# Third stage of an eight-part fused network: routing ahead of the base product, bias as a product, deltas added by accumulating transfers

## The reference, cut to what matters

```
# layer 2 (the third)
y2   = grouped_conv1d(x, 9 taps) + ctx[:, :, None] + bias
base = y2 @ base_w.T + base_b                      # 2048 x 1024 x 1024
h    = y2 @ A.T                                    # rank 64
probs = softmax(y2 @ router_w.T); topw, topi = top_k(probs, 2)
delta = sum over the 2 chosen experts e: topw_e * (h @ B[e].T)     # 16 experts
x    = x + base + 0.5 * delta
# layer 3 (the fourth)
y3 = per-sample 64x64 mix of x + bias
x  = x + layernorm(relu(y3 @ up)**2 @ down + gated latent path) * gamma + beta
```

## Time and profile before

| | us |
|---|---|
| median of 3 runs (lowest to highest) | 1807.75 (1804.79 to 1808.0) |
| profiled execution: its own time | 1816.88 |
| profiled execution: span of the trace | 1815.2 |
| PE busy, share of the span | 1644.1, 91% |
| DVE, ACT, POOL busy | 839.6, 500.3, 423.2 |

### The profile page before, as it was taken

One profiled execution on the slowest core, in us unless ns is written; L12 is line 12 of the kernel. 1 busy time (PEld: TensorE's weight loads), 2 busy tenths in 40 slices (PEclk: granted clock), 3 DMA queues, 4 the chain that ended last, 5 costly groups with the idle time before them and its releaser, 6 DMA issues.

```text
span 1815.2 us, 20711 instructions
## 1 busy us (share of the span) xinstructions
PE 1644.1 (91%) x7830; PEld 1326.3 (73%) x7830; DVE 839.6 (46%) x1294; ACT 500.3 (28%) x763; POOL 423.2 (23%) x272
## 2 busy tenths in 40 slices
PE   6799678999897978776899999999999999999997
PEld 3688546988875646655678888888767888888875
DVE  5455458995274433654523333333282333333326
ACT  2344223333225332110032222221243222222112
POOL 1000111234245244555611111111251111111110
PEclk9999889999997988878999999999999999999999
DMA  8577444457831355455621111111462111111114
GB/s 280 132 176 168 152 77 151 161 179 234 312 141 53 115 214 197 165 187 202 232 91 47 47 47 46 46 46 47 134 214 70 47 47 47 46 46 46 47 58 162
DMA packets 108210, 222.82 MB, mean 123 GB/s; under 512 B 21892, under 2 KB 60924, under 8 KB 107260
## 3 DMA queue, kind: packets, MB, share of 16 engines
q1 hardware_dynamic: 86612, 161.00, 27.9%
q0 software_dynamic: 13120, 38.88, 6.6%
q10 hardware_dynamic: 8400, 21.89, 3.7%
HBM read 152.96 MB, written 76.61 MB: 126 GB/s over the span
## 4 chain that ended last, share of the span: by engine, by line
PE 67%; DMA 7%; DVE 4%; POOL 3%; issue 2%; ACT 2%; SPq 1%; another core or an unknown queue 1%; ACTq 0%; POOLq 0%; DVEq 0%
PE pd L1775 25%; PE pu L1775 24%; PE pf L1775 6%; PE l_po L1775 4%; DMA delta<-scratch_expert_out 3%; PE pw L390 2%; PE pw L391 2%; POOL l_x L1371 1%; PE l_ea L1213 1%; DMA scratch_expert_out<-expert_out,pair_rows 1%; PE l_po L1714 1%; DMA l_y<-scratch_y2T 1%; DMA pair_rows<-scratch_pairs 1%; PE pg L997 1%
## 5 line engine op out<-in xcount | busy, mean ns | idle before, releaser
L1910 POOL TENSOR_TENSOR down_lo<-raw,down_hi 128x1024 fp32r<-128x1024 f32 x40 | 100.3, 2508 | 698.2 <-ACT down_hi L1923 698.2
L1775 PE MATMUL pd<-down_hi,hid_hi 128*128 128x512 f32 x640 | 249.1, 389 | 2.9 <-issue 2.9
L1775 PE MATMUL pu<-y_hi,up_hi 128*128 128x512 f32 x640 | 249.2, 389 | 0.0
L1775 PE MATMUL pu<-y_hi,up_lo 128*128 128x512 f32 x640 | 249.0, 389 | 0.0
L1775 PE MATMUL pd<-down_hi,hid_lo 128*128 128x512 f32 x640 | 249.0, 389 | 0.0
L1775 PE MATMUL pd<-down_lo,hid_hi 128*128 128x512 f32 x640 | 249.0, 389 | 0.0
L1775 PE MATMUL pu<-y_lo,up_hi 128*128 128x512 f32 x640 | 249.0, 389 | 0.0
L2079 DVE TENSOR_TENSOR hid_lo<-hidden,hid_hi 128x512 fp32r<-128x512 f32 x64 | 44.3, 692 | 393.3 <-ACT hid_hi L1987 393.3
L2018 DVE TENSOR_TENSOR acc<-pd,acc 128x512 f32<-128x512 f32 x224 | 143.6, 686 | 54.7 <-PE pd L1775 51.4
L1981 ACT ACTIVATE hidden<-pu 128x512 f32<-128x512 f32 x64 | 38.3, 598 | 464.9 <-PE pu L1775 464.9
L1775 PEld LDWEIGHTS pd<-down_hi,hid_hi 128*128 128x128 f32 x640 | 120.2, 188 | 28.6 <-issue 3.7
(11 more groups left out here) (306 smaller groups left out, 2689.4 us busy)
## 6 DMA issues: line engine op xcount, KB each, us to landing
X<-scratch_x SPq DMA_DIRECT2D x256, 64.0 KB, 2.6
l_x<-scratch_x SPq DMA_DIRECT2D x32, 512.0 KB, 5.8
delta<-scratch_expert_out SPq DMA_DIRECT2D x32, 512.0 KB, 7.2
raw<-in_up SPq DMA_DIRECT2D x32, 512.0 KB, 3.7
raw<-in_down SPq DMA_DIRECT2D x32, 512.0 KB, 4.2
x_in<-in_x SPq DMA_DIRECT2D x16, 512.0 KB, 4.7
scratch_x<-x_in SPq DMA_DIRECT2D x16, 512.0 KB, 4.4
scratch_x<-l_x SPq DMA_DIRECT2D x16, 512.0 KB, 5.6
```

Source lines behind the costliest of these rows:

```text
L1775: mm = pe.matmul(out, lhs[a], rhs[b], start=first and n == 0, stop=last and n == len(pairs) - 1)
L1910: pool.tensor_tensor(dn[u][i][1][:], raw[i][:], dn[u][i][0][:].bitcast(F32), ALU.subtract).then_inc(dn_lo, 1)
```

## The change

**Order.** On PE the last conv tile and the last two router products come ahead of the second half of base tile 0, and `rank_pairs` behind base chunk (1, 0). DVE runs `choose` right after the last conv output. Only base tiles 0 to 5 and the first half of 6 stand ahead of the experts; the second half of tile 6 is spread over the first nine expert groups, three matmuls at a time; nine steps follow, with base tiles 7 to 15, and the mixes start one step later.

**Loads.** `y2` is loaded in halves, the expert matrices in eight pieces of 1 MB by SP instead of four of 2 MB by ACT, and split with one copy per expert instead of two. ACT issues `mats_in`, POOL the stores of y3.

**Experts.** Row numbers travel as floats and are copied out of the group's buffer (`row_numbers`), and the pair rows are copied twice side by side (`pair_rows_twice`), so a group's buffer is free once both copies are made; one transpose of 128 columns replaces a transpose and a matmul. The outputs alternate between two pairs of banks instead of three.

**Bias.** Two matmuls per tile with 33 rows add `base_b` in place of POOL's 16 additions.

**Deltas.** `deltas_in`, `delta_sum` and `add_deltas` are gone. POOL issues two accumulating transfers per tile from the expert rows onto the tile of `x`; from tile 7 on `base_out` comes behind them. Beta is no longer added in this stage but by an accumulating transfer onto the loaded `x3b` slot in the fourth stage.

```diff
+        all_expert_rows(pool)
+        for t in range(NT + 1):
+            if t < NT:
+                if t < 7:
+                    pool.wait_ge(x3p_made, 2 * (t + 1))
+                else:
+                    pool.wait_ge(x3_loaded[t % 4], 16 * (t // 4 + 1))
+                pool.dma_start(x3[t][:], SC["eo"][t * P:(t + 1) * P, :], accum_op=ALU.add).then_inc(first_added[t % 2], 16)
+            if t:
+                last = t - 1
+                pool.wait_ge(first_added[last % 2], 16 * (last // 2 + 1))
+                if last >= 2:
+                    pool.wait_ge(second_added[last % 2], 16 * (last // 2))
+                pool.dma_start(x3[last][:], SC["eo"][(NT + last) * P:(NT + last + 1) * P, :], accum_op=ALU.add).then_inc(
+                    second_added[last % 2], 16)
+            if t >= 13:
+                y3_out(t - 5)
...
         def rows_in(g):
-            n = min(4, NEXP - 4 * g)
             if g >= 3:
-                sp.wait_ge(tr_mm, g - 2)
-                for sem in eo_stored:
-                    sp.wait_ge(sem, 16 * (g - 2))
+                sp.wait_ge(twice, g - 2)
+                sp.wait_ge(row_ids, g - 2)
...
+        def x3_again(t):
+
+            old = t - 9
+            sp.wait_ge(x3b_stored[old % 4], 16 * (old // 4 + 1))
+            sp.wait_ge(y_mm, 2 * (old + 1))
+            x3_in(t)
...
         def base_out(t):
+            dve.wait_ge(x3_loaded[t % 4], 16 * (t // 4 + 1))
             dve.wait_ge(base_mm, 2 * (t + 1))
-            dve.wait_ge(xb, t + 1)
+            if t >= 7:
+                dve.wait_ge(second_added[t % 2], 16 * (t // 2 + 1))
...
+        def base_bias(t):
...
+            for h in range(2):
+                last = pe.matmul(po[t % 2][h][:], K["ones_r"][0:BR, :], brow[:, chunk(h)], start=False, stop=True)
+            last.then_inc(base_mm, 1)
...
         base_chunk(0, 0)
         prior["conv"](pe, NT - 2)
         router(pe, NT - 3)
-        base_chunk(0, 1)
         prior["conv"](pe, NT - 1)
         router(pe, NT - 2)
+        router(pe, NT - 1)
+        base_chunk(0, 1)
         base_chunk(1, 0)
-        router(pe, NT - 1)
+        rank_pairs()
         base_chunk(1, 1)
-        base_chunk(2, 0)
-        rank_pairs()
-        base_chunk(2, 1)
-        for t in range(3, 8):
+        for t in range(2, 6):
             base_chunk(t, 0)
             base_chunk(t, 1)
+        base_chunk(6, 0)
         turn_rows(0)
...
         for g in range(NGRP):
             if g + 1 < NGRP:
                 turn_rows(g + 1)
-            for i in range(4 * g, min(4 * g + 4, NEXP)):
-                expert_tile(i)
-        for b in range(8):
-            if b == 0:
-                pe.wait_ge(eo_act, NEXP)
-                pe.wait_ge(eo_dve, NEXP)
-            base_chunk(8 + b, 0)
-            base_chunk(8 + b, 1)
-            mix(2 * b)
-            mix(2 * b + 1)
+            for n in range(rows_of(g)):
+                expert_tile(4 * g + n)
+            if g == 0:
+                base_start(6, 1)
+            if g < 8:
+                base_part(6, 4 + g // 2, g % 2)
+            if g == 8:
+                base_bias(6)
+        for s in range(9):
+            base_chunk(7 + s, 0)
+            base_chunk(7 + s, 1)
+            for t in mixed_tiles(s):
+                mix(t)
...
+        def add_beta(T):
+            pool.wait_ge(x3b_loaded[T % 2], 16 * (T // 2 + 1))
+            pool.dma_start(x3b[:, T % 2, :], A["L3_ffn_ln_beta"].partition_broadcast(P), accum_op=ALU.add).then_inc(beta_added[T % 2], 16)
...
                     pool.wait_ge(out_made, T + 1)
                     pool.dma_start(tile_of(out, T), acc[:, t, :]).then_inc(out_stored, 16)
+                    if t + 2 < HT:
+                        add_beta(T + 2)
```

More of the change, by code:

```diff
@@ L1141, in phase_l2 @@
 def phase_l2(nc, K, A, SC, s_, buf, first, prior):
[L1146 to L1150, removed]
+    B, B_raw, y2s, y2, war, blank, lg, below, every, pos, expert_of, ids, G, Gd, res, brow, brow_raw, bias_tmp, val, taken, pick = [buf[n] for n in (
+        "B B_raw y2s y2 war blank lg below every pos expert_of ids G Gd res brow brow_raw bias_tmp val taken pick").split()]
+    half_tmp, rT, eo, x3, mats, bias3, y3, y, y_raw, ea, tr, po = [buf[n] for n in (
+        "half_tmp rT eo x3 mats bias3 y3 y y_raw ea tr po").split()]
+    ge, key, lg2, ex, posf, steps, count, steps_int, pair_int, compare, prod = [buf[n] for n in (
+        "ge key lg2 ex posf steps count steps_int pair_int compare prod").split()]
     m, kmax, m2, e2, z, tot, w, tiles, scan1, scan2 = [buf[n] for n in "m kmax m2 e2 z tot w tiles scan1 scan2".split()]
@@ L1156, in phase_l2 @@
     po = [po[0:2], po[2:4]]
-    out_banks = [ea, po[0], po[1]]
+    out_banks = [ea, po[1]]
     py = [ea, tr]
     R1A, R1B, R2A = 15, 23, 36
[L1161 to L1164, removed]
@@ L1288, in sync @@
         sp.wait_ge(r_mm, NT)
+        sp.wait_ge(val_stored, 16 * 2 * NT)
+        for g in range(3):
+            rows_in(g)
+        sp.wait_ge(B_rest, E2)
         x3_in(6)
-        x3_in(7)
[L1291 to L1297, removed]
-        x3_in(8)
@@ L1299, in sync @@
[L1299 to L1306, removed]
-        for b in range(8):
[L1308 to L1313, removed]
+        y2_in(7, 0)
@@ L1314, in sync @@
+        for g in range(3, NGRP):
+            rows_in(g)
+            if g == 6:
+                y2_in(7, 1)
+        y2_in(8, 0)
+        sp.wait_ge(tr_mm, NGRP)
+        x3_in(7)
+        sp.wait_ge(twice, NGRP)
+        sp.wait_ge(row_ids, NGRP)
+        x3_in(8)
+        y2_in(8, 1)
+        for s in range(9):
+            if 9 + s < NT:
+                y2_in(9 + s, 0)
+            elif 9 + s == NT:
                 sp.wait_ge(y2_lo, 2 * NT)
                 first["raw"](sp, 0)
-                sp.wait_ge(xb, NT)
@@ L1666, in tensor, with base_part, base_start @@
     def tensor(pe):
-        def base_chunk(t, c):
+        def base_part(t, k, h):
+            return split_product(pe, po[t % 2][h][:], [v[:, k * P:(k + 1) * P] for v in y2s],
+                                 [v[:, k, chunk(h)] for v in base], k == 0, False)
+        def base_start(t, c):
             if c == 0:
@@ L1697, in turn_rows @@
                 pe.wait_ge(route, R2A)
[L1698 to L1701 removed]
+            for n in range(rows_of(g)):
+                last = pe.transpose(tr[g % 2][:, n * P:(n + 1) * P], Gd[:, g % 2, n, :, :].rearrange("p u r -> p (u r)"), K["ident"][:])
             last.then_inc(tr_mm, 1)
```

442 lines of the change are left out of this document (241 added, 201 removed).

## The result

| | us, median (lowest to highest) | ratio to before, 95% interval |
|---|---|---|
| before | 1807.9 (1804.8 to 1810.2) | |
| changed | 1783.3 (1777.0 to 1785.7) | 0.986 [0.9829, 0.989] |
| forecast | 1728 (range 1695 to 1772) | 0.956 |

What follows compares the result with a forecast made beforehand. PE gaps in the third stage, from waits for `y2` and deltas, were taken as the bound. Third stage -87, fourth +7: -80, 1816.9 to 1737 profiled; with the median 9.1 lower, 1728 us, range 1695 to 1772.

Steps and rivals of the forecast that it cites:

- The fourth stage ... +7: Fourth stage: adding beta between a slot's load and use costs +4 at the first half's end, +3 at the program's end.
- first base chunk: Start of the base work in the third stage, taken at 471.15 us as origin for all new times.
- expert stores, first to last: Third stage, experts: 6.4 to 6.7 us per four tiles, 11.5 times, 75 us against 97.1 before.
- to the end of the stage: Third stage from base tile 9 at 690: 1.5 half clock, 115.5 for seven steps, 6 for DMA, ending at 813.
- step from profile to median: The median of runs taken as 9.1 us below the profiled execution, as in the kernel before.
- the order up to the first scatter: Third stage, start: reordered PE work and earlier `choose` put the first pair scatter at 506.8 us, against 532.5.
- the one stall before base tile 9: Third stage: PE waits 23 us for `y2_low`, queued on DVE behind tile 7's `base_out` and its deltas.
- Gaps in the expert beat: Sign of being wrong: expert stores not keeping the even beat of 6.4 to 6.7 us per four.
- The deltas: Third stage: two accumulating transfers per tile, 4.5 us taken between 2.9 (cost like plain) and 5.9 (cost double).
- A landing of an accumulating transfer beyond 8 us: Sign of being wrong: any accumulating transfer taking over 8 us to land.
- At nothing: POOL's 16 bias and 16 beta additions: Third stage: removing these additions priced at no gain, since only the first tiles' bias was ever waited for.
- PE starving during the scatter: Rival, chance 0.15: PE's wait around the pair scatter returns at some 535 to 550 us, +16, total 1744.

Runs made afterwards that it cites:

- run 1: Changed kernel without the sixteen accumulating transfers of beta, so the output lacks beta; 1744.8 us, ratio to before 0.9542.
- run 4: Kernel before with only beta moved, from POOL's additions in the third stage to accumulating transfers in the fourth; 1831.0 us, ratio to before 1.0022.
- run 6: Changed kernel with beta accumulated onto the stored x3b in DRAM instead of the loaded slot; 1749.2 us, ratio to before 0.9606.
- run 3: Changed kernel with all accumulating transfers (both deltas and beta) made plain, output overwritten and not summed; 1752.7 us, ratio to before 0.9598.
- run 9: Kernel before, unchanged, run again for its trace on another chip; that one execution took 1808.9 us.
- run 5: Changed kernel itself, run again on another chip; 1778.8 us, ratio to before 0.9765.
- run 7: Changed kernel with each tile's second delta loaded plainly and added onto x by POOL; 1773.2 us, ratio to before 0.9727.
- run 10: Changed kernel with second deltas of tiles 0 to 7 issued one place later, three accumulating transfers under way; 1783.7 us, ratio to before 0.9841.
- run 12: Changed kernel, base tiles 7, 8 before deltas, DVE emptying mix banks first, both deltas plain and POOL-added, beta onto stored x3b; 1735.9 us, 0.9582 of before.
- run 11: Changed kernel with base tiles 7 and 8 added before the deltas and DVE emptying mix banks before its base sums; 1762.5 us, ratio to before 0.9733.

## Why the prediction was wrong

The step that failed is **"The fourth stage ... +7"**: beta costs 31 to 32 there (runs 1, 4 and 6), 25 more than forecast. The chain was named, and sized with the wrong numbers. I divided one turn by two slots and compared it with PE's time per tile, "(4.1 + 1.0 + 4 + 1.5)/2 = 5.3". A turn is 13 to 15 us: the load takes 4.0 to 7.0, not 4.1, the accumulating transfer 5.2 to 7.0, not 4, and the very first pair costs 8.1 + 16.15 behind the loads of y3. At 13.5/2 = 6.7 per tile the chain is slower than PE (5.5: 24 of the 168 matmuls in 38.36 us of run 6), so each turn adds, and the start is added whole: from the end of the first half's last upward product to where PE goes on without a wait (1236.07 to 1304.69), 49.1 us became 68.6, 19.5 more where I had 4. At the end of the program I priced one tile behind the last load (+3); the chain there holds three turns, 7.0 + 6.6, 6.4 + 5.2 and 4.0 + 5.4, and costs the other 12.5. That the transfers accumulate is the smaller part: made plain they still leave 26 of the 32 us (run 3).

The other terms, in the trace:

| step | forecast | after | difference |
|---|---|---|---|
| first base chunk | 471.2 | 479.1 | +7.9 |
| to the first pair scatter | 35.7 | 36.0 | +0.4 |
| to the first expert store | 58.2 | 59.6 | +1.4 |
| expert stores, first to last | 75 | 79.4 | +4.4 |
| to base tile 9 | 50 | 55.6 | +5.6 |
| to the end of the stage | 123 | 122.6 | -0.4 |
| fourth stage, against before | +7 | +32.0 | +25.0 |

That is 44.5 us before rounding. Another 10.8 lie in the step from profile to median: the profile of before stood 9.1 above its median, that of the changed kernel 1.6 below. Together the 55 us missed. The shown execution of the kernel before held the wait behind the scatter that run 9 lacks, so its 9.1 us above the median need not hold for another kernel.

**Right**: the order up to the first scatter; the expert beat over the first ten groups (6.1 to 7.0 us per four stores, 6.6 on average); the one stall before base tile 9 and its mechanism, though 29.9 us for 23; the loop at PE's own speed, its steps 15.35 us each where 16.5 to 18 were forecast. These shorter steps paid for a wait of 10.45 us for the first matrices that I had not seen, so that the forecast 123 was met is partly luck. (The 18 was also a slip: 7 MB at 358 GB/s are 19.6 us. The two bias matmuls took 0.67 us, between my 0.45 and 0.9.)

**The expert cycle** missed by 4.4 us, and 3.4 of them are one gap, the eleventh group's 9.9 us. "Gaps in the expert beat" was one of my signs of being wrong:

```profile
645.27 0.69 DVE L1632 COPY expert_out<-l_ea 128x512 f32<-128x512 f32 x1 [4.42 <-DMA scratch_expert_out<-expert_out,pair_ids]
646.80 0.98 POOL L1372 DMA_INDIRECT scratch_expert_out<-expert_out,pair_ids  x1 [3.93 <-DVE expert_out L1632]
```

The copies out of PSUM wait for an output buffer whose scatter has not landed. SP had issued two loads of `x` of 512 KB each at 636.5, ahead of it. The gap stands before the same 43rd store in runs 1, 3, 5, 7 and 10; that these loads make it is likely and untested.

**The deltas**, 4.5 us a tile, measured 5.2. The Trainium skill ("Collectives: The Full Stack", The bandwidth ceiling) has a reducing transfer at half a copy's rate. The traces agree nearly: 198 GB/s at a share of 1.01 in the changed kernel against 296 at 0.82 in run 3, so 361 full by estimate, a factor of 1.8. I had both ends, 2.9 and 5.9, and took the middle; the plain pair took 3.3 and the accumulating one 5.2, nearer to the upper end. "A landing of an accumulating transfer beyond 8 us" was another of my signs of being wrong, and it came: 9.1 us in the median, 14.4 at most.

**"At nothing: POOL's 16 bias and 16 beta additions"** was wrong of the kernel before: run 4 shows the 16 beta additions at 27 us. The bias additions were not tried alone. It didn't hurt the sum, which was built forward and not by difference.

**The start.** Nothing shows the 7.9 us at the first base chunk to be an effect of the change: over all traces it starts between 471.0 and 482.4 in the kernel before and between 473.5 and 482.8 in the changed ones. I had taken the earliest of them as the origin.

**PE starving during the scatter** did not come back in any trace of the changed kernel. In the shown execution PE has 21 matmuls in the 20 us from 560, in run 4 20 in those from 570, in run 9 90. The row of 15.56 us names no releaser; that base tile 5 was behind it was my reading of the code. What makes it, and why it is in two of the three traces of the kernel before and its variant, stays open; so does the share of it in the 24.6 us, which on another chip were 43 (run 5).

## What to carry to other kernels

Adding by transfer frees an engine and lengthens a chain. Price load + transfer + use against the bound engine's time per item, times the number of slots; take the landings of that stretch and not of a quiet one, and count the first turn whole. If the operand is stored somewhere in between, accumulate onto the stored copy while the transfer engines idle; that took 30.6 of the 32 us away (run 6 against run 5). An addition that stays on POOL has a second price where DVE works beside it on two SBUF operands (run 12). An origin taken from one execution carries its luck into every later number.

## What the runs showed of the hardware

- Accumulating transfers of 512 KB from DRAM onto SBUF fill the 16 engines at 198 GB/s (changed kernel); plain ones on the same queue run at 296 with 0.82 of them (run 3). A third under way only lengthens the landings, 9.1 to 11.4 us in the median (run 10).
- On POOL the record of such an issue lasts 0.83 to 1.2 us, that of a plain one 0.53 where no transfer accumulates (run 3) and 0.69 to 1.23 between accumulating ones (run 7). The next issue that waits for nothing starts 0.52 to 0.73 us behind it in all three, so the longer record is not time lost.
- Beside additions on POOL, DVE's fp32 subtractions of two SBUF operands take longer: 128x1024 3.3 us instead of 1.2, 128x512 2.5 instead of 0.7 (medians, run 12 against run 11).
- An accumulating transfer with DRAM at both ends and a source broadcast over 128 rows lands after 6.7 to 11.4 us, and sixteen of them left F within 1 us of the run without them, at a DMA share of 0.19 (run 6, 850 to 1200 us).
